# A decoder layer's expert rows: transposed by TensorE, or split first and transposed by one DMA per slot

## What is computed

```python
x = x + self_attention(layernorm(x))            # one causal head with a linear bias
x = x + cross_attention(layernorm(x), ctx)      # 16 heads of 16
h = layernorm(x)
p = softmax(h @ w_gate); keep the top 2 of 8 experts, normalised
g, u = split(h @ w_gate_up[e])                  # 256 -> 2 * 1024, for each expert e
x = x + sum over the 2 chosen experts of p[e] * ((silu(g) * u) @ w_down[e])
```

## Time and profile before

| what | value |
|---|---|
| three executions | 1104.51, 1108.24, 1108.52 us |
| span of the profiled execution, first to last instruction | 1101.4 us |
| the profiled execution's own time | not given; its span is 6.8 us below the median of the three |
| TensorE busy | 1042.1 us, 95% of the span |
| VectorE, ScalarE, GpSimd busy | 666.3, 654.7, 522.1 us |
| mean granted TensorE clock | 0.990 |
| moved by DMA | 142.76 MB, 130 GB/s over the span |

### The profile page before, as it was taken

How to read it: one execution, slowest core, us unless ns; L and a number is a source line. 1 busy time by engine, 2 the same in 40 slices (tenths; PEclk the granted TensorE clock), 3 DMA queues, 4 the chain that set the end, 5 groups by cost and what they waited for, 6 DMA issues and landing times.

```text
span 1101.4 us, 36849 instructions
## 1 busy us (share of the span) xinstructions
PE 1042.1 (95%) x12742; PEld 884.4 (80%) x12742; DVE 666.3 (60%) x2153; ACT 654.7 (59%) x1439; POOL 522.1 (47%) x563
## 2 busy tenths in 40 slices
PE   4789999999999999889999999999999999999996
PEld 2457677777777776548899999999999999999996
DVE  5667788888888887854564444444444444444443
ACT  6588889888888888664443443444344344344332
POOL 4756677777777777423352332324323323323322
PEclk9899999999999999999999999999999999999999
DMA  5754666666666663386222451294221221238211
GB/s 181 238 187 161 170 174 176 172 181 181 179 182 181 183 183 108 107 297 232 45 37 36 143 152 29 46 393 113 33 34 29 33 33 29 37 100 297 42 29 20
DMA packets 91943, 142.76 MB, mean 130 GB/s; under 512 B 21232, under 2 KB 69808, under 8 KB 88560
## 3 DMA queue, kind: packets, MB, share of 16 engines
q1 hardware_dynamic: 76062, 122.96, 35.8%
q0 software_dynamic: 15808, 19.09, 10.7%
q10 hardware_dynamic: 18, 0.01, 0.0%
HBM read 268.13 MB, written 43.47 MB: 283 GB/s over the span
## 4 chain that ended last, share of the span: by engine, by line
PE 83%; DVE 6%; SPq 3%; ACT 3%; issue 2%; DMA 2%; POOL 1%; DVEq 0%; ACTq 0%; POOLq 0%
PE front L2307 17%; PE t_ring L2307 17%; PE s_ring L2325 8%; PE pv L2325 8%; PE pv L2022 5%; PE s_ring L1989 5%; PE t_ring L2007 5%; PE front L1864 4%; PE s_ring L1851 2%; PE front L1873 2%; PE front L1922 2%; PE tail L1873 2%; DVE nmax L1284 2%; PE tail L1851 1%; PE front L1851 1%
## 5 line engine op out<-in xcount | busy, mean ns | idle before, releaser
L787 POOL DMA_INDIRECT out<-y_sb,place_i x71 | 112.3, 1582 | 316.9 <-DVE y_sb L1761 121.9
L2307 PE MATMUL front<-rows_hi,wgu_sb 128*128 128x128 f16 x2272 | 213.5, 219 | 1.6 <-DVE rows_lo L1736 1.6
L2307 PE MATMUL t_ring<-rows_hi,wgu_sb 128*128 128x128 f16 x2272 | 214.6, 220 | 0.0
L1284 DVE TENSOR_REDUCE nmax<-s_ring 128x2 f32<-128x512 f32 x256 | 167.5, 682 | 53.7 <-PE s_ring L1989 52.5
L2307 PE MATMUL t_ring<-rows_lo,wgu_sb 128*128 128x128 f16 x1136 | 198.6, 220 | 0.0
L2307 PE MATMUL front<-rows_lo,wgu_sb 128*128 128x128 f16 x1136 | 197.6, 219 | 0.0
L2307 PEld LDWEIGHTS front<-rows_hi,wgu_sb 128*128 128x128 f16 x2272 | 180.5, 98 | 4.1 <-DVE rows_lo L1736 2.1
L2307 PEld LDWEIGHTS t_ring<-rows_hi,wgu_sb 128*128 128x128 f16 x2272 | 181.3, 98 | 1.6
L954 ACT ACTIVATE probs_t<-t_ring,mask_bias 128x512 f32<-128x512 f32 x256 | 167.1, 705 | 22.4 <-PE t_ring L2007 20.3
L1144 ACT ACTIVATE silu_g<-t_ring 128x256 f32<-128x256 f32 x142 | 54.6, 385 | 167.8 <-PE t_ring L2307 167.8
L1792 DVE SCALAR_TENSOR_TENSOR act_t<-t_ring,silu_g 128x256 f32<-128x256 f32 x142 | 60.3, 425 | 152.2 <-ACT silu_g L1144 152.2
(11 more groups left out here) (248 smaller groups left out, 2100.6 us busy)
## 6 DMA issues: line engine op xcount, KB each, us to landing
wgu_sb<-gu_split SPq DMA_DIRECT2D x71, 2048.0 KB
wd_sb<-down_split SPq DMA_DIRECT2D x71, 1024.0 KB
w_piece<-in_w_gu SPq DMA_DIRECT2D x32, 512.0 KB, 6.4
gu_split<-w_halves SPq DMA_DIRECT2D x32, 512.0 KB, 3.8
w_piece<-in_w_down SPq DMA_DIRECT2D x16, 512.0 KB, 7.6
down_split<-w_halves SPq DMA_DIRECT2D x16, 512.0 KB, 5.2
x_in<-in_x SPq DMA_DIRECT2D x16, 256.0 KB
ctx_in<-in_ctx_t_in SPq DMA_DIRECT2D x16, 256.0 KB
```

The costliest lines, as they stand in the source:

```text
L787: nc.gpsimd.indirect_dma_start(out=out, out_offset=bass.IndirectOffsetOnAxis(ap=place_i[:, j:j + 1], axis=0), in_=y_sb[:, j], in_offset=No ...
L1284: nc.vector.tensor_reduce(nmax[:, n // HJ, :, n % HJ], s_ring[n % 2][:].rearrange("p (r k) -> p r k", r=2), AX.X, ALU.max, negate=True).th ...
L2307: o = nc.tensor.matmul(gu_ring[f][:, part * SLOT:(part + 1) * SLOT], wgu_sb[j][:, w, at:at + P], r[:, j % 2, c], start=(i == 0), stop=(i = ...
```

## The change

ScalarE and VectorE now split the gathered rows in SBUF, before any transpose, into `rows_h` (128 rows, by 2 slots in turn, by 2 halves, by 256 columns, fp16). SP then issues one transposing DMA per slot (`rows_turn`), SBUF to SBUF, 128 x 512 fp16 to `rows_t` (four 128x128 blocks: 2 halves by 2 chunks; 128 KB), with four buffers. TensorE's transposes and their bank are gone; its slot waits for `rows_turned[j]`. The splits run two slots ahead in round 1, not one. The gather of slot s + 4 waits for `rlo_sb` of slot s in place of `rt_ps`. In `last_attention` ScalarE rounds slot 0's rows after g = 2 (before: g = 3) and slot 1's after g = 5; VectorE's rest of slot 1 follows `t_norm3`. The sizes and values of the matrix products are unchanged. The core of the diff:

```diff
-        rows_hi = sb("rows_hi", [P, 2, NC, SLOT], F16)
-        rows_lo = sb("rows_lo", [P, 2, NC, SLOT], F16)
+        rows_t = sb("rows_t", [P, STREAMS, 2, NC, SLOT], F16)
+        rows_h = sb("rows_h", [P, 2, 2, D], F16)
...
+            def rows_turn(s, j):
+                sp.wait_ge(rlo_sb, s + 1)
+                if not isinstance(s, int) or s >= STREAMS:
+                    sp.wait_ge(gu_ps, FP * (s - STREAMS + 1))
+                sp.sem_inc(sync_passed, 1)
+                sp.dma_start_transpose(rows_t[:, j].rearrange("p a c n -> p (a c) n"),
+                                       rows_h[:, j % 2].rearrange("p a d -> p (a d)")).then_inc(rows_turned[j], 16)
...
                 load_gate_up(e, j)
                 load_down(e, j)
+            rows_turn(0, 0)
             iteration(15, 1, 7, True, True, False, False, False)
+            for j in range(1, STREAMS):
+                rows_turn(j, j)
             store_stream(B - 1)
             store_normed(B - 1, 1)
 
-            def slot(s, j, weights, ahead):
-
+            def slot(s, j, weights, ahead, turned=True):
+
+                if turned:
+                    rows_turn(s + 2, (j + 2) % STREAMS)
                 if weights:
                     e, new = expert(s + STREAMS), other(s + STREAMS)
                     sp.wait_ge(gu_ps, FP * s + FP)
...
             for s in range(2 * STREAMS):
-                slot(s, s % STREAMS, True, True)
+                slot(s, s % STREAMS, True, True, s >= 2)
...
-                    pool.wait_ge(rt_ps, s - STREAMS + 1)
+                    pool.wait_ge(rlo_sb, s - STREAMS + 1)
...
-            def rows_round(s, p):
-                act.wait_ge(rt_ps, s + 1)
-                nc.scalar.activation(rows_hi[:, p], rows_bank[:, 0:D].rearrange("p (c n) -> p c n", c=NC), ACT.Copy,
-                                     scale=RSCALE).then_inc(rhi_sb, 1)
+            def rows_round(s, j, g):
+                act.wait_ge(rows_in[j], 16 * g + 16)
+                if not isinstance(s, int) or s >= 2:
+                    act.wait_ge(rows_turned[j - 2], 16 * (g if j >= 2 else g - 1) + 16)
+                nc.scalar.activation(rows_h[:, j % 2, HI], rows[:, j], ACT.Copy, scale=RSCALE).then_inc(rhi_sb, 1)
...
-                        rows_round(s + 1, 1 - j % 2)
+                        rows_round(s + 2, (j + 2) % STREAMS, g + (j + 2) // STREAMS)
...
-                    if g == 3:
-                        rows_round(0, 0)
+                    if g == 2:
+                        rows_round(0, 0, 0)
+                    if g == 5:
+                        rows_round(1, 1, 0)
...
+                nc.vector.scalar_tensor_tensor(rows_h[:, j % 2, LO], rows[:, j], RSCALE, rows_h[:, j % 2, HI],
+                                               ALU.mult, ALU.subtract).then_inc(rlo_sb, 1)
...
-            def rows_transposed(s, j, g):
...
-                                             r[:, j % 2, c], start=(i == 0), stop=(i == len(products) - 1))
+                                             rows_t[:, j, r, c], start=(i == 0), stop=(i == len(products) - 1))
...
-                    pe.wait_ge(rlo_sb, s + 1)
+                    pe.wait_ge(rows_turned[j], 16 * g + 16)
                     pe.wait_ge(wgu_in[j], 16 * g + 16)
...
-                    if ahead and f == 1:
-                        rows_transposed(s + 1, (j + 1) % STREAMS, g + (j + 1) // STREAMS)
...
-                        rows_transposed(0, 0, 0)
...
                     if g == 4:
-                        pe.wait_ge(rlo_sb, 1)
+                        pe.wait_ge(rows_turned[0], 16)
                         pe.wait_ge(wgu_in[0], 16)
                         gate_up(0, 0, 0)
```

More of the change, by code:

```diff
@@ L276, in decoder_layer @@
         down_banks = [s_ring[0], pv]
-        rows_bank = s_ring[1]
         consts_loaded, slope_loaded, gate_loaded = map(sem, "consts_loaded slope_loaded gate_loaded".split())
@@ L319, in decoder_layer @@
         rows_in, wgu_in, wd_in = sems("rows_in", STREAMS), sems("wgu_in", STREAMS), sems("wd_in", STREAMS)
-        rt_ps, rhi_sb, rlo_sb, gu_ps, silu_sb, act_sb = map(
-            sem, "rt_ps rhi_sb rlo_sb gu_ps silu_sb act_sb".split())
+        rows_turned = sems("rows_turned", STREAMS)
+        rhi_sb, rlo_sb, gu_ps, silu_sb, act_sb = map(sem, "rhi_sb rlo_sb gu_ps silu_sb act_sb".split())
         ahi_sb, alo_sb, down_ps, y0_sb, y1_sb, act_used = map(sem, "ahi_sb alo_sb down_ps y0_sb y1_sb act_used".split())
         zeroed, pads_out, stream_out, k_zeroed, ones_set = map(sem, "zeroed pads_out stream_out k_zeroed ones_set".split())
-        act_passed, vec_passed, pool_passed = map(sem, "act_passed vec_passed pool_passed".split())
+        act_passed, vec_passed, pool_passed, sync_passed = map(
+            sem, "act_passed vec_passed pool_passed sync_passed".split())
         block = stack.enter_context(nc.Block())
@@ L593, in _ @@
                 slot(s, s % STREAMS, True, False)
+            for s in range(NSLOT - STREAMS, NSLOT - 2):
+                slot(s, s % STREAMS, False, False)
         @block.gpsimd
@@ L1136, in last_tail, with slot @@
                     t_gate(B - 1)
-            def slot(s, j, ahead):
+            def slot(s, j, g, ahead):
                 first = isinstance(s, int) and s == 0
@@ L1177, in _ @@
             for s in range(2 * STREAMS):
-                slot(s, s % STREAMS, True)
+                slot(s, s % STREAMS, s // STREAMS, True)
             with act.Fori(2, GROUPS - 1) as g:
                 for j in range(STREAMS):
-                    slot(STREAMS * g + j, j, True)
+                    slot(STREAMS * g + j, j, g, True)
             for s in range(TABLE - STREAMS, NSLOT):
-                slot(s, s % STREAMS, s + 1 < NSLOT)
+                slot(s, s % STREAMS, s // STREAMS, s + 2 < NSLOT)
             result(NSLOT - 1, (NSLOT - 1) % STREAMS)
@@ L1732, in late_table, with rows_rest @@
                                             ).then_inc(table_sb, 1)
-            def rows_rest(s, p):
+            def rows_rest(s, j):
                 vec.wait_ge(rhi_sb, s + 1)
-                nc.vector.scalar_tensor_tensor(rows_lo[:, p], rows_bank[:, 0:D].rearrange("p (c n) -> p c n", c=NC),
-                                               RSCALE, rows_hi[:, p], ALU.mult, ALU.subtract).then_inc(rlo_sb, 1)
+                nc.vector.scalar_tensor_tensor(rows_h[:, j % 2, LO], rows[:, j], RSCALE, rows_h[:, j % 2, HI],
+                                               ALU.mult, ALU.subtract).then_inc(rlo_sb, 1)
             def act_rest(s, f):
@@ L1797, in slot @@
                     if f == 1 and ahead:
-                        rows_rest(s + 1, 1 - j % 2)
+                        rows_rest(s + 2, (j + 2) % STREAMS)
                     last = isinstance(s, int) and s == NSLOT - 1
@@ L1833, in last_attention @@
                 t_norm3(b - 1, 0, b // 2)
+                rows_rest(1, 1)
                 t_logits(b - 1)
@@ L1844, in _ @@
             for s in range(TABLE - STREAMS, NSLOT):
-                slot(s, s % STREAMS, s // STREAMS, False, s + 1 < NSLOT)
+                slot(s, s % STREAMS, s // STREAMS, False, s + 2 < NSLOT)
         @block.tensor
@@ L2279, in _ @@
             attention_loop(pe, first_fronts, iteration)
-            def rows_transposed(s, j, g):
-                pe.wait_ge(rows_in[j], 16 * g + 16)
-                if isinstance(s, int) and s == 0:
-                    pe.wait_ge(on_sb, 2 * B - 2)
-                else:
-                    pe.wait_ge(rlo_sb, s)
-                for c in range(NC):
-                    o = transpose(rows_bank[:, c * P:(c + 1) * P], rows[:, j, c * P:(c + 1) * P])
-                o.then_inc(rt_ps, 1)
             def gate_up(s, j, f):
@@ L2301, in gate_up @@
                     pe.wait_ge(exp_sb, 16 * B - 3 + f)
-                products = [(c, w, r) for c in range(NC) for w, r in ((HI, rows_hi), (HI, rows_lo), (LO, rows_hi))]
+                products = [(c, w, r) for c in range(NC) for w, r in ((HI, HI), (HI, LO), (LO, HI))]
                 for part in range(4):
@@ L2346, in last_tail, with slot @@
                     t_rank(B - 1)
-            def slot(s, j, g, ahead):
+            def slot(s, j, g):
                 if not isinstance(s, int) or s > 0:
-                    pe.wait_ge(rlo_sb, s + 1)
+                    pe.wait_ge(rows_turned[j], 16 * g + 16)
                     pe.wait_ge(wgu_in[j], 16 * g + 16)
@@ L2397, in _ @@
             for s in range(2 * STREAMS):
-                slot(s, s % STREAMS, s // STREAMS, True)
+                slot(s, s % STREAMS, s // STREAMS)
             with pe.Fori(2, GROUPS - 1) as g:
                 for j in range(STREAMS):
-                    slot(STREAMS * g + j, j, g, True)
+                    slot(STREAMS * g + j, j, g)
             for s in range(TABLE - STREAMS, NSLOT):
-                slot(s, s % STREAMS, s // STREAMS, s + 1 < NSLOT)
+                slot(s, s % STREAMS, s // STREAMS)
             for f in range(FP - 2, FP):
```

## The result

| | before | after |
|---|---|---|
| median of 4 executions each | 1107.07 us | 1116.93 us (1113.13 to 1125.06) |
| ratio after to before | | 1.0107, 95% interval 1.0079 to 1.0134 |
| profiled execution | | 1113.13 us |
| its span | 1101.4 us | 1111.3 us |
| mean granted clock of its span | 0.990 | 0.981 |

By the medians the change made the kernel 9.9 us slower; the ratio on record, 1.0107, is 11.8 us. The forecast was 14.4 us slower, 1122.6 us, with a range of 1111 to 1136. The profiled executions are near the fastest of each kernel, and their spans differ by 9.9 us too.

The account below looks back on a forecast made before the run. TensorE's stream was taken to bound slots 8 to 70. Terms -15.2 + 22.7 + 1.5 + 2.9 + 1.5 + 1.0 = +14.4 us on 1108.2 gave 1122.6 us; own range 1115 to 1131, 8 in 10 1111 to 1136.

Parts of the forecast that it names:

- The pair: TensorE's two transposes per slot, 0.22 us in its stream, 71 pairs: removing them gains 15.2 us.
- Stall 1: At slot 0 the transpose queues behind 10.5 MB of weights on SP, lands at 514.1; TensorE loses 22.7 us.
- rival A: Slot 0's transpose does not wait behind the weights and lands at 496.8: 1101.8 us in all; chance 0.13.
- Rival B: Slow transposes, 11.2 us each, lengthen both stalls, the reload burst and clock loss: 1146 us; chance 0.10.
- Rival C: Stalls half as long, as weights drain faster or the attention behind catches up: near 1109 us; chance 0.05.
- Clock: After each of the two stalls a lower granted clock slows TensorE's next products: 1.5 us each.
- Stall 2: At slot 4 SP issues the transpose only after batch 15's stores and slots 0 and 1: 2.9 us lost.
- Weight reloads: From 714 to 750 us four streams change expert; transposes behind the loads land late: 1 us, 0 to 9.
- moved at no cost: Row splits and gathers, needed a slot earlier, still fit their slack: no cost to TensorE.

Follow-up runs that it names:

- turn0_w1: The changed kernel with slot 0's transposing DMA issued after slot 1's weights, before those of slots 2 and 3: 1106.51 us, ratio 0.9996 to the kernel before.
- turn0_w2: The changed kernel with slot 0's transposing DMA issued after slot 2's weights, before slot 3's: 1110.58 us, ratio 1.005 to the kernel before.
- turn0_act: The changed kernel with slot 0's transposing DMA issued by ScalarE on its own queue, SP's next transposes waiting for its end: 1116.02 us, one execution.
- turn0_turn4: The changed kernel with slot 0's transpose after slot 1's weights and slot 4's ahead of batch 15's stores: 1101.52 us, ratio 0.9967 to the kernel before.
- before_turns: The kernel before, TensorE's transposes kept, plus a transposing DMA per slot that nobody computes with: 1110.79 us, ratio 1.0042 to the kernel before.
- spread_gu5_gather: The changed kernel with early transposes moved, slot 0's round 0 after g = 5, gathers issued ahead of results: 1111.92 us, ratio 1.0049 to the kernel before.

## Why the prediction was right, and where it was off

**The pair, -15.2 us: right.** Two readings: 15.6 us by itself (interval 11.5 to 19.8), and -13.9 from slot 8 on with -1.0 before it. Slots take 7.98 us, as forecast. The 390 ns per transpose of the Trainium skill ("VectorE: DVE Perf Modes", "The three transpose paths") would have made the gain 55 us, an estimate. The distance between starts in the trace decided.

**Stall 1, +22.7 us: the mechanism right, the size off.** The first expert product moved from 491.42 to 509.27, by 17.9 us (the wait grew by 18.5 and TensorE came to it 0.7 sooner). The error is all in the landing: 509.2, not 514.1. Of these 4.9 us, 1.4 are that the loads began sooner (first down load at 478.74, before at 480.17) and 0.7 that the transfer took 2.3 us, not 3. The other 2.8 us are in what went through ahead of it: my slices were those of before, where the kernel's other work shared the DMA engines. From 480.2 to 511.1 us of before GpSimd's queue moved 0.40 MB in 11.08; from 478.7 to 506.9 us of after it moved 0.13 in 10.42. And 500 to 505 us ran at 403 GB/s and at 431 with all compute engines standing still. I put the 1.4 us down to chance: in the profiled executions on record the first down load is issued anywhere from 478.7 to 484.5 us.

The argument behind it, that SP's queue serves in order, is borne out by the packets of the kernel after: those of the transpose go when the weights are through. turn0_w1 and turn0_w2 show that fewer weights ahead mean a sooner landing. That the transpose would do better with a queue of its own, the basis of **rival A** (1101.8 us), is what turn0_act excludes: 18.7 us in place of 5.4. The gather that I took for evidence ran beside one 2 MB load; here there were 10.5 MB, and the transpose has 544 packets where GpSimd's queue shows 48 from 473 to 480 us of before, when that gather ran. **Rival B** fell with the 2.3 us landing. The estimate of 5.2 us from the Trainium skill's 1309 ns ("VectorE: DVE Perf Modes", "The three transpose paths") was more than twice what the transpose took. The statement of the Trainium skill's page "Advanced Engine Details and Errata", "X-Bar Transpose (TRN2)", that it is as fast as a regular DMA holds roughly when the queue is empty: 2.3 us against 1.7 for the plain store. **Rival C** came in small part: the weights did drain faster, but stall 1 kept 17.9 of 22.7 us.

**Clock: the first 1.5 us right** (1.7 us measured, 1.2 of it in the 24 products, granted clock 0.75 from 510 to 515 us). **The second 1.5 us wrong:** after the 2.44 us wait at slot 4 the 24 products ran at the higher level (granted clock 1.00 from 555 to 560 us). I had taken both from one wait of before of nearly the same length; the waits differ in what TensorE did before them. From 490 to 500 us of before it had been busy 8.2 of 10 us; from 535 to 555 us of after, 19.5 of 20. What exactly the chip goes by is not settled.

**Stall 2, +2.9 us: right** at 2.4 us. turn0_turn4 removed the wait by SP's order alone.

**Weight reloads, +1.0 us: off; 2.9 us, and by another route.** I priced late transposes and put the gathers under "moved at no cost": "The bound 9.2 still fits" and "Nothing here reaches TensorE". That step failed. I compared a gather's own landing time with the slack, and left out what GpSimd has queued ahead of the gather: result DMAs that take over 10 us in the burst, and a wait for an older one. before_turns showed that the traffic alone costs nothing there, which leaves the shorter slack. The route that I priced exists as well: in turn0_w1 the same stretch lost 2.8 us to late transposes. Which of the two comes last differs from run to run, and no run separates what each would cost alone.

From 480 to 485 us, ahead of the first wait, the granted clock was 0.50 against 0.71 before. I forecast nothing for that, and no experiment was aimed at it; TensorE still came to its wait 0.7 us sooner.

In all: -13.9 - 1.0 + 18.5 - 0.7 + 1.7 + 2.4 + 2.9 = +9.9 us, where +14.4 was forecast. The other 1.2 us to 1122.6 are the median of before, 1107.1 with a fourth execution. It is luck in part that the total is not further off: stall 1 and the second clock loss came out 6.3 us smaller than forecast, and the gather that I had left out gave 1.9 us back. The lower end of the forecast's own range, 1115 us, doesn't follow from its terms: 1.7 us to landing and no clock loss give -15.2 + 21.4 + 1.6 + 1.0 = +8.8, or 1117 us.

## What to carry to other kernels

A DMA that replaces compute costs what its queue holds at each place where it is awaited. Look for the places where megabytes stand ahead of it: here two moves in program order turned a ratio of 1.0107 into 0.9967. A queue of its own is no way out while they are in flight. When work is moved earlier by a slot, compare the slack with the time of what feeds it including everything ahead in the feeding engine's program order, not with that feeder's own duration. Here this was read in the trace of one execution, and the run that was aimed at it, spread_gu5_gather, failed for another reason.

## What the runs showed of the hardware

- A queue of its own does not protect a small DMA from megabytes in flight. Beside the 2 MB and 1 MB weight loads 128 KB landed after 10.8 us in 128 pieces and 19.0 us in 512 pieces, and the transpose (544 packets) after 18.7 us, one execution each; the median transpose takes 2.3 us. The two queues took turns packet by packet, 308 to 308 from 498 to 506 us of turn0_act.
- A transposing DMA of 128 x 512 fp16 occupies SP's issue for 1.2 us, against 0.3 to 0.4 us for a plain one (SP's rows above), and moves its 128 KB in 544 packets.
- A result DMA that adds into DRAM took 10.9 us from 737.90 us on, during the reloads, when the DMA engines moved 342 GB/s in all.
- Of two waits of nearly the same length, 2.48 us in the kernel before lowered the granted clock (0.76 from 500 to 505 us), and 2.44 us in the kernel after did not slow the next 24 products (1.51 us).
